# Two attention layers on one core: the ten value steps of a group spread among the scores

## What is computed

```python
x = x + attn_a(layernorm(x), w_qkv_a, w_o_a)
x = x + ffn(layernorm(x), kernel, scale)       # scale * (x @ (2*kernel - 1))
x = x + attn_b(layernorm(x), w_qkv_b, w_o_b)
x = x + ffn(layernorm(x), kernel, scale)
# attention: 32 query heads of 16, 8 key/value heads, rotary embedding,
scores = einsum('bhsd,bhtd->bhst', q, repeat(k, 4)) / sqrt(16)
probs  = softmax(where(causal, scores, -inf))
out    = einsum('bhst,bhtd->bhsd', probs, repeat(v, 4))
```

## Time and profile before

| what | us |
|---|---|
| median of three executions | 1472.55 (1471.66 to 1473.81) |
| profiled execution | 1479.44 |
| its span, first to last instruction | 1477.5 |

### The profile page before, as it was taken

How to read it: one execution, slowest core, us unless ns; L and a number is a source line. 1 busy time by engine, 2 the same in 40 slices (tenths; PEclk the granted TensorE clock), 3 DMA queues, 4 the chain that set the end, 5 groups by cost and what they waited for, 6 DMA issues and landing times.

```text
span 1477.5 us, 28606 instructions
## 1 busy us (share of the span) xinstructions
PE 1352.1 (92%) x11076; PEld 792.2 (54%) x11076; DVE 1040.3 (70%) x1526; ACT 942.1 (64%) x1770; POOL 383.2 (26%) x591
## 2 busy tenths in 40 slices
PE   5989999999998999999999899999998889999998
PEld 4864444446775444444777544444477744444456
DVE  5667888845667788883665688888266578888737
ACT  4646776774663677777556377777655547677754
POOL 3421222210442222211144222222123412222211
PEclk9978999999997999999999699999999989999999
DMA  3000000001000000000220000000010000000002
GB/s 119 1 1 10 9 10 10 3 2 43 1 1 2 9 10 17 2 2 2 86 72 1 2 10 17 10 2 3 2 43 1 1 2 17 10 10 2 3 1 100
DMA packets 12981, 24.00 MB, mean 16 GB/s; under 512 B 1072, under 2 KB 4144, under 8 KB 12848
## 3 DMA queue, kind: packets, MB, share of 16 engines
q1 hardware_dynamic: 12848, 22.19, 4.5%
HBM read 16.94 MB, written 4.19 MB: 14 GB/s over the span
## 4 chain that ended last, share of the span: by engine, by line
PE 70%; DVE 16%; issue 6%; ACT 5%; POOL 2%; DMA 1%; DVEq 0%; SPq 0%; ACTq 0%; POOLq 0%
PE psO L688 20%; PE psE L667 14%; PE psM L625 12%; PE psM L552 12%; DVE mx L1058 8%; PE psE L605 3%; PE psM L535 3%; PE psO L605 3%; PE psM L632 2%; DVE stats L973 2%; ACT probs L895 1%; POOL attn L1202 1%; PE psM L652 1%; DVE attn L1084 1%; DVE qT L1023 1%
## 5 line engine op out<-in xcount | busy, mean ns | idle before, releaser
L895 ACT ACTIVATE probs<-psE 128x512 f32<-128x512 f32 x1152 | 625.3, 596 | 287.7 <-PE psE L667 281.0
L1058 DVE TENSOR_REDUCE mx<-psM 128x2 f32<-128x768 f32 (+4 forms) x704 | 693.1, 1025 | 130.4 <-PE psM L632 103.9
L625 PE MATMUL psM<-kT,qT 48*128 48x384 f32 (+5 forms) x1536 | 316.0, 426 | 49.4 <-DVE mx L1058 35.7
L688 PE MATMUL psO<-probs,v_grp 128*32 128x512 f32 (+3 forms) x3072 | 326.8, 515 | 0.0
L667 PE MATMUL psE<-qT,kT 50*128 50x512 f32 (+3 forms) x1536 | 294.8, 422 | 15.0 <-ACT probs L895 9.5
L1255 POOL TENSOR_SCALAR_AFFINE_SELECT probs<-probs 128x512 f32<-128x512 f32 x256 | 159.3, 634 | 569.3 <-ACT probs L895 532.3
L625 PEld LDWEIGHTS psM<-kT,qT 48*128 48x128 f32 x1536 | 154.0, 197 | 163.5 <-DVE mx L1058 117.9
L667 PEld LDWEIGHTS psE<-qT,kT 50*128 50x128 f32 x1536 | 134.8, 193 | 172.3 <-ACT probs L895 127.4
L632 PE MATMUL psM<-mask_b 64*128 64x64 bf16 x2048 | 124.4, 202 | 0.0
L688 PEld LDWEIGHTS psO<-probs,v_grp 128*32 128x32 f32 x3072 | 68.8, 110 | 93.1 <-issue 72.9
L552 PE MATMUL psM<-wq_hi,xT_hi 128*128 128x512 f32 (+1 forms) x384 | 99.1, 380 | 15.8 <-ACT vs L859 9.5
(11 more groups left out here) (81 smaller groups left out, 1259.5 us busy)
## 6 DMA issues: line engine op xcount, KB each, us to landing
probs<-in_w_qkv SPq DMA_DIRECT2D x5, 1536.0 KB, 6.6
xs<-in_x SPq DMA_DIRECT2D x8, 512.0 KB, 4.0
xn<-in_w_o SPq DMA_DIRECT2D x16, 256.0 KB, 2.6
out_x<-xs SPq DMA_DIRECT2D x8, 512.0 KB, 2.8
qT<-nm_rows SPq DMA_DIRECT2D x128, 8.0 KB
probs<-in_w_ffn SPq DMA_DIRECT2D x1, 256.0 KB, 8.2
attn<-in_mask SPq DMA_DIRECT2D x1, 160.0 KB, 7.8
sin_s<-in_sin SPq DMA_DIRECT2D x1, 128.0 KB, 7.9
```

The lines of the kernel that those rows point to most:

```text
L625: return pe.matmul(psM[:, 2 * pair + h % 2, to:to + k1 - k0], qT[lo:lo + MAXROW, g, qt // QT_PER_CHUNK, h // 2, qt % QT_PER_CHUNK * P:(qt ...
L688: ins = pe.matmul(psO[VW * j:VW * (j + 1), off:off + w], v_grp[:, kb, :], probs[:, (g * NS + s) % PSLOTS, at(j), to:to + w], start=s in (0 ...
L895: act.activation(probs[:, (g * NS + s) % PSLOTS, at(heads[0]):at(heads[0]) + len(heads), 0:w], psE[:, n % SRING, 0:w * len(heads)].rearran ...
L1058: dve.tensor_reduce(to, src, AX.X, ALU.max, negate=True).then_inc(ring_used.sem, 1)
```

## The change

Only the text of GROUP_ORDER is different. PV.9.-1 goes from ahead of N.1.0 to behind U.3. PV.1 to PV.7 each stand one to three places earlier or later, and PV.0 goes ahead of S.4. Three of these moves leave other things next to each other: PV.7 now stands ahead of S.17, so S.17 is followed by S.0 of the next group; PV.5 stands behind S.12 and not behind S.13; O.1.-1 goes from behind S.6 to between U.8 and U.9; and N.0.1, which followed S.14 ahead of U.18, now has U.18 ahead of it.

```diff
 GROUP_ORDER = """
-S.0 U.0 U.1 PV.8.-1 S.1 U.2 PV.9.-1 N.1.0 S.2 OC.1.-1 U.3 U.4 U.5
-S.3 U.6 S.4 PV.0.0 U.7
-S.5 U.8 PV.1.0 U.9 S.6 O.1.-1 OC.0.0 PV.2.0 S.7 U.10 O.0.0
-S.8 U.11 U.12 S.9 PV.3.0 U.13
-S.10 U.14 PV.4.0 S.11 U.15 U.16 S.12 U.17
-S.13 PV.5.0 S.14 N.0.1 U.18 S.15 U.19 PV.6.0
-S.16 U.20 U.21 S.17 PV.7.0 X
+S.0 U.0 U.1 PV.8.-1 S.1 U.2 N.1.0 S.2 U.3 PV.9.-1 OC.1.-1 U.4 U.5
+S.3 U.6 PV.0.0 S.4 U.7
+S.5 PV.1.0 U.8 O.1.-1 U.9 S.6 PV.2.0 OC.0.0 U.10 S.7 O.0.0
+S.8 U.11 PV.3.0 U.12 S.9 U.13
+S.10 PV.4.0 U.14 S.11 U.15 U.16 S.12 PV.5.0 U.17
+S.13 U.18 S.14 N.0.1 U.19 PV.6.0 S.15 U.20
+S.16 U.21 PV.7.0 S.17 X
 """
```

## The result

The changed kernel takes 1662.77 us (median of four, 1646.33 to 1665.89); the kernel before took 1473.18 in the same comparison. The ratio is 1.126, with an interval of 1.118 to 1.134: 190 us slower. Forecast were 1563 us, with a range of 1510 to 1600. The sign was right, and the time lies well outside the range. Half of the loss was forecast; the rest of this text is about the other half.

The account below looks back on a forecast made before the run. PE bounds a group, DVE close behind; only PE's idle time can change. New waits of 3.29 us in 24 middle groups (79 us) and 2.9 in four first groups (12 us) sum to 91 us: 1472.55 becomes 1563, range 1510 to 1600.

Parts of the forecast that it names:

- the three intervals: Distances any order must leave room for: between two S, from a U to its freed banks, from S.6 to O.0.
- The pace of the scores: Two S can never start closer than 1.17 to 1.25 us; with less work between them PE idles.
- The turn of a pair: A pair of psM banks is free 1.80 us after a wide U starts, about 1.25 for U.8, 1.5 for U.14.
- the copy of the outputs: OC.0 runs behind S.6's exponentials, so O.0 can start no sooner than 2.35 us after S.6.
- The head nets to nothing: S.0 to U.6: PV.9.-1 behind U.3 removes U.5's 0.8 us wait, yet U.4's reduction starts no earlier; net 0.
- The sum of waits: Net new PE waits over a middle group: 3.29 us, taking it from 27.92 to 31.2 us.
- signs of being wrong: DVE starting U.4 sooner, ring waits missing, or half clock taking over whole groups; PE's busy time should stay within 1%.
- the likeliest case: Whole kernel: 1563 us from waits alone, with no term for more clock falls; chance 0.55.
- the clock rival: Each middle group gets a half-clock stretch of 1.5 us: 27 to 33 us on top, about 1593; chance 0.18.
- Only the pace counts: DVE and ACT might be ahead at U.9, U.16, U.19 and O.0; 1.6 us a group remain, about 1518; chance 0.18.
- Faster: U.4's reduction starts earlier, so U.5, U.6 and S.4 lose up to 1.2 us of waits a group; 1439; chance 0.05.
- Nothing: Waits only change places, since PE's and DVE's totals are the same: 1472 us; chance 0.04.

Follow-up runs that it names:

- e2_head: The kernel before with only PV.9.-1 moved behind U.3; 1467.1 us, ratio 0.990.
- e7_fill_before: The kernel before with useless matmuls in two stops, two ahead of U.5 and one ahead of U.6; 1483.9 us, ratio 1.000.
- e4_fill: The changed kernel with useless matmuls filling PE's stops, order and waits of other work the same; 1593.5 us, ratio 1.074.
- e3_s17_back: The changed kernel with PV.7 put back behind S.17, stops not filled; 1702.0 us (profiled 1666.9), ratio 1.150.
- e8_line3: The kernel before with PV.1 ahead of U.8, O.1.-1 between U.8 and U.9, PV.2 ahead of U.10 and S.7; 1546.1 us, ratio 1.048.
- e9_ring: The kernel before with only N.0.1 moved behind U.18, so U.19 takes U.18's pair of banks; 1503.8 us, ratio 1.019.

## Why the prediction was wrong

**What bounds the group, and the three intervals: right.** PE at full clock is as busy as before, and all loss at full clock is idle time. The pace of the scores was given as 1.17 to 1.25; the two S at the boundary are 1.29 apart in the trace (653.27 to 654.56), those of the other pairs 1.16 to 1.35. The turn of a pair and the copy of the outputs explain the stops at U.9, U.16, U.19 and O.0.

**The head nets to nothing: right in size, wrong in what it is worth.** Full-clock groups of e2_head are 0.09 us shorter. I priced that part by the length of its stop alone. The order of before also loses the clock in six of 20 groups, that of the head in none, and the prediction had the row for it in hand. That it is the stop at U.5 which costs it is not shown: e7_fill_before fills it, and the clock still falls.

**The sum of waits, 3.29 us a group: low by a fifth.** The measured full-clock group has 4.16 more. Starts against S.0 (502.85 before, 622.47 after) tell which terms were short:

| stretch | forecast | measured |
|---|---|---|
| S.0 to U.6 | 0 | 0.23 |
| U.6 to S.5 | 0.27 | 0.47 |
| S.5 to S.8 | 0.75 | 1.01 |
| S.8 to S.14 | 0.67 | 1.00 |
| S.14 to S.0 | 1.60 | 1.45 |
| sum | 3.29 | 4.16 |

The first is the handover from U.4 to its reduction. I had its start at 5.56 us after S.0 and found it at 5.78. N.1.0 and U.3 wait as worked out, but U.4 is 0.1 later, and DVE starts 0.62 behind it, not 0.5:

```profile
660.34 2.36 DVE L1058 TENSOR_REDUCE mx<-psM 128x2 f32<-128x1024 f32 x2 [0.55 <-PE psM L632]
```

(DVE's timeline; U.4 itself starts at 659.72.) The other differences, 0.2 to 0.3 each, lie where a value step now parts an S and a U that followed each other: S to U costs 0.31 and S to a value step 0.44, and I counted this for S.5 and U.8 only, and left it out of the sum even there. That this is all of it, I only argue; no run takes it apart. Over the 24 middle groups it makes 21 us. The first groups of a round, by what is left of e4_fill's time, take about 7 us more each where I took 2.9, which is 16 us, and by the estimate above some 14 of these are clock, not waits; and filling gave back the 9 us of falls that the kernel before had. 91 + 21 + 16 - 9 is 119, against the 120 (or 112) of e4_fill. Of the 100 us by which 1563 was missed, the terms of waits that were too short make a fifth.

**The clock: the step that failed.** The sum that gave 1563 has no term for it. It was a rival at 0.18 with 27 to 33 us on top of what the kernel before loses; measured are 69 against the filled kernel, so 60 counted in that way, and the first groups' share comes on top. The signs of being wrong that the prediction wrote down for it came: PE's busy time grew by 6% where it was to stay within 1%, and half clock took the larger part of some groups (22 of 39.33 us). Two of its premises fell. First, I took one half-clock stretch of 1.5 us for each group, the only size that the trace of before shows in middle groups. In the changed kernel a stretch can last: from 576 to 602 us the clock stands at half with PE busy for 94% of it, and the group takes 38.49. A lone stretch of 3.4 us still costs 1.45 (33.5 against 32.07), but the 24 distances behind the first of a round are 64 us longer than in e4_fill, 2.7 each. Second, I held against it that PE's work at half clock hides the waits, so each fall would cost less. For the waits for DVE that is so: between 576 and 602 us none is left. Of the stops for ACT three are, and the largest is as long as at full clock, since nothing of PE's lies in it: S.17, exponential, S.0. The other two, S.16 and S.5, are 0.33 and 0.45 us. S.0 in that stretch, timeline of PE:

```profile
584.04 0.80 PE L667 MATMUL psE<-qT,kT 50*128 50x512 f32 x2 [0.79 <-ACT probs L895]
```

And the likeliest case should not have been one without more falls: in six of 20 groups the trace of before had a fall behind a cluster of about 1.3 us of stops by starts, and the new order makes three such clusters a group (U.6 with S.5, S.14 to S.16, S.0 to U.3). Clusters are a warning and no rule: most groups of before have the same one and no fall, and taking S.0's stop away (e3_s17_back) did not lessen the time at half clock. The range ended at 1600 since it took the clock rival's central value and not what happens when stretches join.

**The other rivals.** "Only the pace counts" is out: the ring waits stand in the trace, and e8_line3 and e9_ring make them one by one. "Faster" decided at U.3, and U.3 waits for U.2's reduction, 3.72 us after S.0; e2_head shows the group unchanged. "Nothing" is out.

The Trainium skill (TensorE: Matmul & The Clock Gate, "Why this matters for your kernels") ties a fall of the clock to idle gaps several times longer than any here. The longest stop in a full-clock group of the changed kernel is 0.78 us, and filling such stops kept the clock up there (e4_fill); so the measurement decides against using that rule as a safe bound. The section "A second HAM failure mode: psum-queue depth-cycling" of the same page of the Trainium skill tells of micro-idles between groups of matmuls, frequent enough for the clock to swing. The changed kernel's trace agrees (eleven stops, 5.7 us of a group); that of e7_fill_before, which falls with PE busy for 3.84 of 4.00 us, does not.

## What to carry to other kernels

In an order written by hand, look for the distances that a reader must leave open (matmul, then exponential, then the next matmul into that ring; product, then reduction, then the next product into that bank) and for what fills each; "spread evenly" takes the filler out of some of them. A list from which banks are dealt in turns is part of the order: to swap two entries can pair a job with its neighbour. Where PE is over nine tenths busy, price each stop twice, once by its length and once by what it does to the clock. A version with the stops filled by useless matmuls tells the two apart where the filling does take the falls away, as it did in the changed order and did not in that of before. Moving one stop can be worth more than its length, as in the head of this change, or less, as in e3_s17_back: take the time at half clock from the trace each time.

## What the runs showed of the hardware that I had not expected

Adding 520 matmuls that do nothing made a kernel 69 us faster (11076 to 11596 on PE, 1662.8 to 1593.5 us), since the clock stayed at 2.4 GHz in the middle groups. Once at half, the clock did not come back for 26 us (576 to 602), with PE 94% busy by the profile; these runs don't say what brings it back. Nor do they say what brings it down: in e7_fill_before it fell with PE busy for 96% of the 4 us before. With stops unfilled the same kernel differs by 20 us between executions (1646 to 1666), and e3_s17_back by 47 (1667 to 1714), while e2_head, whose middle groups have no fall in its trace, stays within 4 us (1466.3 to 1469.9) and e4_fill, whose don't either, differs by 10.
